# Reordering the last feed-forward unit ahead of an expert loop

## What is computed

```python
n = layernorm(x)                              # x: 2048 tokens x 256
y = layernorm(n + attention(n, n, n, causal)) # one head, 2048 x 2048, d = 256
y = layernorm(y + attention(y, ctx, ctx))     # ctx: 1601 rows
y = layernorm(y + relu(y @ w1 + b1) @ w2 + b2)  # 256 -> 1024 -> 256
x = x + y
h = layernorm(x)                              # then 8 experts, 2 per token
p, i = top_k(softmax(h @ wg.T), 2)            # gates p normalised to 1
x = x + sum_over_chosen(p * (silu(h @ w1[e].T) * (h @ w3[e].T)) @ w2[e].T)
```

## Time and profile before

| | |
|---|---|
| median of 3 runs | 534.37 us (532.86 to 537.04) |
| profiled execution, its own time | 529.8 us |
| its span, first to last instruction | 527.9 us |
| mean granted clock of TensorE | 0.994 of full |
| TensorE busy | 497.2 us, 94% |
| VectorE busy | 377.3 us, 71% |
| ScalarE busy | 286.2 us, 54% |
| GpSimd busy | 287.9 us, 55% |

### The profile page before, as it was taken

How to read it: one execution, slowest core, us unless ns; L and a number is a source line. 1 busy time by engine, 2 the same in 40 slices (tenths; PEclk the granted TensorE clock), 3 DMA queues, 4 the chain that set the end, 5 groups by cost and what they waited for, 6 DMA issues and landing times.

```text
span 527.9 us, 10992 instructions
## 1 busy us (share of the span) xinstructions
PE 497.2 (94%) x3686; PEld 325.3 (62%) x3686; DVE 377.3 (71%) x968; ACT 286.2 (54%) x575; POOL 287.9 (55%) x324
## 2 busy tenths in 40 slices
PE   7899999999899999898999999899999799999992
PEld 3576766666566666665757676646566466666661
DVE  5899887588867669867888889888858644444441
ACT  4556867646466745664655855864454243344430
POOL 4463213003832708955599586447565566677773
PEclk9999999999999999999999999999999999999997
DMA  8002534246789337784496962147779567888893
GB/s 259 32 32 70 170 101 118 83 106 106 138 177 161 102 77 171 136 173 141 86 175 162 205 189 93 60 111 110 112 153 141 89 120 130 120 143 130 134 116 40
DMA packets 135314, 65.61 MB, mean 124 GB/s; under 512 B 109757, under 2 KB 126590, under 8 KB 135262
## 3 DMA queue, kind: packets, MB, share of 16 engines
q1 hardware_dynamic: 127774, 54.69, 48.4%
q0 software_dynamic: 7488, 10.23, 12.7%
HBM read 28.19 MB, written 10.35 MB: 73 GB/s over the span
## 4 chain that ended last, share of the span: by engine, by line
PE 61%; DVE 13%; POOL 8%; ACT 6%; DMA 6%; issue 3%; SPq 1%; POOLq 0%; ACTq 0%; DVEq 0%
PE ps L1203 50%; PE ps L1298 3%; DMA probT<-prob 3%; PE ps L1300 2%; PE ps L1299 2%; DVE cmax L1740 2%; PE ps L1529 2%; ACT ps L1013 1%; DMA y<-hrow,qst 1%; POOL nrm L783 1%; ACT prob L1012 1%; POOL tT L891 1%; POOL y L840 1%; ACT tT L999 1%; DVE prob L1881 1%
## 5 line engine op out<-in xcount | busy, mean ns | idle before, releaser
L1203 PE MATMUL ps<-arena,probT 128*128 128x256 f16 (+2 forms) x1092 | 180.0, 318 | 4.8 <-DMA probT<-prob 2.4
L1203 PEld LDWEIGHTS ps<-arena,probT 128*128 128x128 f16 (+1 forms) x1092 | 104.6, 97 | 62.0 <-issue 9.2
L964 POOL DMA_INDIRECT out<-y,qst x39 | 62.5, 1602 | 17.9 <-DMA out<-y,qst 9.4
L1203 PE MATMUL ps<-arena,qT 128*128 128x512 f16 (+1 forms) x384 | 68.9, 332 | 1.6 <-DVE prob L1881 1.2
L2299 DVE SCALAR_TENSOR_TENSOR ps<-ps,w1m 128x512 f32<-128x512 f32 x39 | 27.3, 699 | 57.1 <-ACT w1m L1142 54.4
L1012 ACT ACTIVATE prob<-ps,nbias 128x512 f16<-128x512 f32 x64 | 38.9, 609 | 53.3 <-DVE nbias L1746 53.3
L1142 ACT ACTIVATE w1m<-ps 128x512 f32<-128x512 f32 x39 | 23.3, 597 | 77.6 <-PE ps L1203 62.9
L1203 PE MATMUL ps<-arena,tT 128*128 x468 | 57.4, 273 | 0.7 <-DVE tT L2400 0.6
L779 POOL TENSOR_TENSOR rstd<-veps,expo 128x1 f32<-128x1 f32 x16 | 9.6, 599 | 88.3 <-DVE veps L1775 88.3
L1203 PEld LDWEIGHTS ps<-arena,qT 128*128 128x128 f16 x384 | 32.4, 97 | 37.1 <-issue 3.2
L938 POOL DMA_INDIRECT y<-hrow,qst x39 | 40.1, 1028 | 19.8 <-issue 9.9
(11 more groups left out here) (233 smaller groups left out, 916.4 us busy)
## 6 DMA issues: line engine op xcount, KB each, us to landing
stage<-we_in SPq DMA_DIRECT2D x33, 256.0 KB, 3.1
prob<-we_in SPq DMA_DIRECT2D x15, 256.0 KB, 3.8
xin<-x_in SPq DMA_DIRECT2D x16, 128.0 KB, 2.7
out<-y SPq DMA_DIRECT2D x16, 128.0 KB
hrow<-tT SPq DMA_DIRECT2D x4, 512.0 KB, 3.7
y<-x_in SPq DMA_DIRECT2D x3, 512.0 KB, 7.6
stage<-z_in SPq DMA_DIRECT2D x4, 256.0 KB, 5.8
prob<-w_in SPq DMA_DIRECT2D x4, 256.0 KB, 2.8
```

The costliest lines, as they stand in the source:

```text
L964: g.indirect_dma_start(out[:rows_of(p), :], bass.IndirectOffsetOnAxis(ridx[:, n:n + 1], 0), ys[:, n % RING, :], None, compute_op=ALU.add). ...
L1203: r = t.matmul(o, lhs(a), rhs(b), start=first and n == 0, stop=last and n == 2)
```

## The change

No matmul, transfer or gather is added or dropped. Most edits change only the order of an engine's list.

- `last_norm`: the first step of the norm of the last cross-attention tile (subtract the mean, multiply) moves from GpSimd to VectorE.
- GpSimd: `out_adds(2)` moves behind `gather(0)` and `gather(1)`.
- ScalarE: `out_scaled(2)` moves from behind `relu(3, 2)` to behind `relu(3, 6)`. The load of the Silu table moves behind `x_copy(0)` and `x_copy(1)`, and `silu(0)` ahead of `h_hi(2)`.
- TensorE: `make_lists(0)` ahead of `up(3, 6)`. `x_trans(0)` ahead of `down(3, 6)`, `x_trans(1)` ahead of `down(3, 7)`.
- VectorE: block 2's output tiles and the first low parts ahead of `table_keys(0)`, `list_read(0)` at once behind `hid_lo(3, 5)`, `centre(2)` around it, low parts of the rest later, `h_lo(2)` behind `gated(0)`.
- The 13 rest pieces are sorted so that the 8 with w1 and w3 come ahead of the 5 with w2.
- `e_ups(0)` waits for those 8 only, and the first `e_downs` for all 13.
- REST_AT places the high parts of the rest differently on ScalarE.

```diff
-        rest = [n for n in rest if n >= in_zT] + [n for n in rest if n < in_zT]
-        R_ZT = NE * NP - in_zT
+        rest = sorted(rest, key=lambda n: (n % NP >= 2 * KD, n < in_zT))
+        R_ZT = [n < in_zT for n in rest].index(True)
+        R_UPS = [n % NP >= 2 * KD for n in rest].index(True)
         REST_AT = {2: {5: (0,), 6: (1, 2), 7: (3,)},
-                   3: {0: (4,), 1: (5,), 2: (6,), 3: (7, 8), 4: (9,), 5: (10,), 6: (11,), 7: (12,)}}
+                   3: {0: (4,), 1: (5,), 2: (6,), 3: (7,), 4: (8,), 5: (9, 10), 7: (11, 12)}}
...
             def ln_affine(pre, i, q, row):
-                pool.wait_ge(sm[pre + "rstd"], i + 1)
-                g.tensor_scalar(nrm[:, q, :], u[:, q, :], mv[:, q, 0:1], rstd[:, q, :], ALU.subtract,
-                                ALU.mult).then_inc(sm[pre + "nrm"], 1)
+                if i < NT - 1:
+                    pool.wait_ge(sm[pre + "rstd"], i + 1)
+                    g.tensor_scalar(nrm[:, q, :], u[:, q, :], mv[:, q, 0:1], rstd[:, q, :], ALU.subtract,
+                                    ALU.mult).then_inc(sm[pre + "nrm"], 1)
...
-            out_adds(2)
...
             gather(0)
             gather(1)
+            out_adds(2)
             rstd_of("m_", 2)
...
-                    if u == NB - 1 and f == 2:
+                    if u == NB - 1 and f == 6:
                         out_scaled(2)
...
-            a.activation(shift[:], shift[:], ACT.Silu)
...
             x_copy(1, 1)
+            a.activation(shift[:], shift[:], ACT.Silu)
+            silu(0, 0)
             h_hi(2)
-            silu(0, 0)
...
+            make_lists(0)
             up(3, 6)
-            make_lists(0)
             down(3, 4)
             up(3, 7)
             down(3, 5)
+            wait(pe, "f_lo", KF * NB - 2)
+            x_trans(0, 0)
             down(3, 6)
+            wait(pe, "f_lo", KF * NB - 1)
+            x_trans(1, 1)
             wait(pe, "r_tab", 1)
             expert_of(0)
             down(3, 7)
-            wait(pe, "f_lo", KF * NB - 2)
-            x_trans(0, 0)
-            wait(pe, "f_lo", KF * NB - 1)
-            x_trans(1, 1)
             wait(pe, "f_lo", KF * NB)
-            wait(pe, "st_lo", G_FF + len(rest))
+            wait(pe, "st_lo", G_FF + R_UPS)
...
                 if n == BEHIND:
                     wait(pe, "r_lg", NB - 1)
+                    wait(pe, "st_lo", G_FF + len(rest))
...
+            def last_norm():
+
+                wait(dve, "c_y", NT - 1)
+                wait(dve, "c_rstd", NT)
+                v.tensor_scalar(nrm[:, 1, :], u[:, 1, :], mv[:, 1, 0:1], rstd[:, 1, :], ALU.subtract,
+                                ALU.mult).then_inc(sm["c_nrm"], 1)
...
             rest_los(2, 5)
+            last_norm()
             table_starts(0)
...
-            table_keys(0)
             for m in range(TB):
                 out_tile(2, m)
+            for m in range(TB - 1):
+                out_stats(2, m)
             hid_lo(3, 0)
-            for m in range(TB):
-                out_stats(2, m)
+            out_stats(2, TB - 1)
             out_moments(2)
             hid_lo(3, 1)
+            table_keys(0)
+            hid_lo(3, 2)
             table_experts(0)
-            rest_los(3, 0)
-            hid_lo(3, 2)
-            centre(2, range(TB))
+            hid_lo(3, 3)
             rows_hot(1)
-            hid_lo(3, 3)
+            hid_lo(3, 4)
             tiles_hot(0)
             spread_vals(0)
-            rest_los(3, 1)
-            hid_lo(3, 4)
-            rest_los(3, 2)
-            rest_los(3, 3)
+            centre(2, (0, 1))
             hid_lo(3, 5)
             list_read(0)
-            rest_los(3, 4)
+            centre(2, (2, 3))
+            rest_lo(dve, 4)
+            rest_lo(dve, 5)
+            rest_lo(dve, 6)
             hid_lo(3, 6)
-            rest_los(3, 5)
+            rest_lo(dve, 7)
+            rest_lo(dve, 8)
             hid_lo(3, 7)
+            rest_lo(dve, 9)
             for m in range(TB):
                 x1_stats(2, m)
             x1_aggr(2)
-            rest_los(3, 6)
-            rest_los(3, 7)
             for m in range(TB):
                 out_tile(NB - 1, m)
+            rest_lo(dve, 10)
             h_norm(2)
             table_rest(0)
-            h_lo(2)
...
             gated(0, 0)
+            h_lo(2)
             act_lo(0, 0)
+            rest_lo(dve, 11)
             gated(1, 1)
...
             out_moments(j)
+            rest_lo(dve, 12)
```

## The result

The changed kernel takes 535.41 us (median of 20 runs), the kernel before 532.97 us (20 runs). The ratio is 1.0052, with a 95% interval of 1.0031 to 1.0074, so about 2.8 us slower. The ratio is taken over the fast executions: it leaves out two of the changed kernel's 20, at 540.30 and 1336.53 us. The median of before is 1.4 us lower here than that of the three runs shown earlier. The profiled execution of the changed kernel has a span of 533.3 us.

A forecast was written before the change was run, and what follows sets the result against it. TensorE, with 61% of the chain of waits, was taken to bound it. The 3.6 us gained at e_ups(0) turn idle before x_trans(2), 0.3 us later: 534.37 + 0.3 = 534.7 us, range 532.0 to 538.3.

The forecast's parts named there:

- main step: TensorE's turn to the experts: 3.6 us gained at e_ups(0) become idle time before x_trans(2), which starts 0.3 us later.
- the adds took under 3 us: GpSimd's four adds of out_adds(2): a sum under 3 us would show the part on the adds wrong.
- the clock of 0.5 in the first expert tiles: TensorE's granted clock: 0.5 in the first expert tiles would show the forecast wrong altogether.
- low end: x_trans(2) with the low bounds, 2.9 us of adds and 2.77 us of landing: 0.9 us earlier.
- `last_norm`, 0.44 us gained: Norm step moved from GpSimd to VectorE: 0.88 us earlier, so TensorE's 0.44 us wait before y_trans(3) goes.
- Idle times of 0.52 and 0.60 us, and the lists: TensorE in unit 3: waits for low parts of pieces 0 and 3 go; make_lists(0) starts at 332.2, r_list at 333.3.
- Rival 3: The list comes no earlier than before, at 337.7, so x_trans(2) is 4.7 us later: 539.1 us, chance 0.1.
- Rival 1: The gain stays, x_trans(2) held only by unit 3's output tiles and starting at 343.5: 530.8 us, chance 0.08.
- `gather(0)` and `gather(1)`: First two gathers on GpSimd start at 334.2 and 335.8 and land at 337.0 and 338.6.
- `out_adds(2)`: Four adds on GpSimd start at 337.1 and take 3.6 us, between 2.9 and 4.28; n_x1 at 340.7.
- `gather(2)`: Third gather on GpSimd, behind moments and rstd, starts at 344.4; landing of 3.0 us puts x_trans(2) at 347.4.
- Rival 2, the clock: TensorE's clock falls in the 3.9 us hole before x_trans(2), costing 2.3 us: 537.0 us, chance 0.2.

The follow-up runs named there:

- e2: Changed kernel with gather(2) moved ahead of out_adds(2) on GpSimd, nothing else; ratio to the kernel before 1.0007.
- e9: Changed kernel with block 2's sum early (centre(2), out_scaled(2), out_adds(2) moved forward) and gather(2) ahead of rstd_of("m_", 2); ratio to the kernel before 0.9933.
- e6: Changed kernel with centre(2) ahead of hid_lo(3,3), out_scaled(2) behind relu(3,3), out_adds(2) ahead of gather(0); ratio to the kernel before 0.9978.
- e7: Kernel before with only the last_norm step moved to VectorE; one execution, no ratio given.
- e5: Changed kernel with out_adds(2) on 8 of 256 columns, leaving out most of that addition; ratio to the kernel before 1.0018.
- e1: Changed kernel with 14 extra matmuls of 512 columns in TensorE's hole between e_ups(0) and x_trans(2); ratio to the kernel before 1.0053.
- e4: Changed kernel with out_adds(2) ahead of gather(0) again, out_scaled(2) still behind relu(3,6); ratio to the kernel before 1.0087.

## Why the prediction held, and where its steps were off

It said no change within 1%, 0.3 us slower, with a range of 532.0 to 538.3. The ratio is 0.5% up and the time is in the range. Its main step held: the gain at `e_ups(0)` is swallowed by a hole ahead of `x_trans(2)`, since `gather(2)` stands behind block 2's sum. e2 and e9 show that by taking that order away, e6 by taking away the late sum.

That 535.41 lies only 0.7 us above the forecast of 534.7 is luck. The forecast was counted from the median of three runs, 534.37, and the kernel before is at 532.97. The change itself cost about 2.8 us where 0.3 was forecast. By its own signs the prediction failed in part: the adds took under 3 us, and the clock of 0.5 in the first expert tiles, which it had called wrong altogether, came in the profiled execution. Its low end was also added up wrong: 2.9 us for the adds and 2.77 for the landing give `x_trans(2)` at 346.5, which is 0.6 us earlier than 347.08, and not 0.9.

By its own steps, in times less 1.31:

- *`last_norm`, 0.44 us gained.* Wrong. `y_trans(3)` started at 315.88, where 315.27 was forecast. I had seen that VectorE would wait with `table_starts` and one low part behind it, costed that at nothing, and looked only at the next low part, not at the one that `y_trans(3)` itself waits for. e7 shows the term alone.
- *Idle times of 0.52 and 0.60 us, and the lists.* Right: both gone, lists at 332.4 for 332.2, r_list at 333.6 for 333.3. Rival 3 (the list isn't earlier) fell. Rival 1 fell too: `x_trans(2)` waited 3.2 us for the gather.
- *`gather(0)` and `gather(1)`.* 334.5 and 336.4 for 334.2 and 335.8.
- *`out_adds(2)`.* I took 3.6 us, between 2.9 and 4.28. It took 2.77, each add 0.72 to 0.74. The step that failed is beside it: I let VectorE's low parts hold up the adds, from the row in which VectorE's `centre` and `rows_hot` did, and did not ask what the adds would do to VectorE. It went the other way, at 2.7 us for one low part (3.42 for 0.68). That made 1.42 us ahead of `down(3, 7)`, so `e_ups(0)` came at 342.7 for 340.9, and it put `x1_stats(2)` at 341.9 for 340.7. e5 shows it.
- *`gather(2)`.* At 345.2 for 344.4, for that reason. TensorE went on 3.5 us after its start, where I took 3.0 and bounded it by 3.26. GpSimd's own part of that gather took 1.51 us where it took 1.02 before. Why is open. `x_trans(2)` came at 348.7 for 347.4, which is 1.6 us later than before and within the 2.3 us allowed.
- *Rival 2, the clock.* It came on top in the profile: `e_ups(1)` took 3.96 us and not 2.6, 1.4 us of the 2.3 that I had priced. 1.6 + 1.4 = 3.0 us in this profile, beside the 2.8 us of the ratio. How often it falls in the timed executions the runs don't show (e1).

The Trainium skill ("SBUF — State Buffer", "SBUF: two separate sides") has it that, of a VectorE operation with two SBUF inputs and a GpSimd operation that reads SBUF, whichever starts first gets their shared port pair for the whole instruction, and the other waits. The traces agree that the two hold each other up. e2 agrees in full: the low part started 0.07 us behind the first add and took 1.27 us, about one add more. The changed kernel does not: there the low part started 0.09 us ahead of the first add, so by the rule it would have taken its 0.68 us, and it waited for all four adds. The measurement decides.

## What to carry to other kernels

When a consumer is moved earlier, walk on to the next one that shares its queue: the third gather stood behind the sum that the first two had been put ahead of, so the gain became a hole. Cost a contended pair of operations in both directions, and put the elementwise work of a side engine where the other side has nothing urgent. If a wait is taken from one engine, list every semaphore that the waiting instruction asks for, since the gain ends where the second latest of them comes.

## What the hardware did that I had not expected

- One low part on VectorE (two SBUF operands) that started 0.1 us ahead of four adds of GpSimd took 3.42 us instead of 0.68. e1 repeats it at 3.41. In e2, where it started just behind the first add, it took 1.27 us and the adds 3.29 instead of 2.77. In e4 the same two kinds met and the adds took 4.21 us, and two low parts 1.82 us instead of 1.29. The kernel before shows the other side: its first add started at 328.87, ahead of `rows_hot` at 329.23, and took 2.165 us, until 0.6 us after `rows_hot` had ended. Which side pays changed from run to run with the order of arrival. No run varied that alone.
- The clock fell in a turn where TensorE had only short idle times. In e7 two waits of 0.80 and 0.99 us stood within 2.5 us that held only two short `x_trans`, and the clock was 0.62 over 344 to 346 and 0.52 over 346 to 348. In the profile of before the same turn kept 1.00.

```profile
342.00:344.00 2.00, 0.45 (x6) 0.24 (x4) 2.00 (x6) 1.19 (x2) 1.81 (x2) 1.00 0.06 23
344.00:346.00 2.00, 1.77 (x5) 0.74 (x6) 1.97 (x9) 0.31 (x1) 1.53 (x2) 0.62 0.22 66
346.00:348.00 2.00, 2.00 (x6) 0.73 (x5) 1.67 (x5) 0.74 (x1) 0.95 (x1) 0.52 0.34 92
```

`e_ups(0)` took 4.29 us there and 2.60 in the profile of before. So a single profile can carry 1.7 us of clock that another execution with the same order in that turn does not have.
